# A router computed with its weights as the stationary operand, and its steps and the base downs in another order

## The reference

```
h = layernorm(x)*(1+ca) + sa
x = x + ga * (attention(layernorm(h)*gamma+beta) @ o_proj + h)      # causal, one head of 256
h = layernorm(x)*(1+cb) + sb
gate, up = h @ Wg.T, h @ Wu.T                                        # 704 wide
probs = softmax(h @ Wr.T); topw, topi = top_k(probs, 2)              # the router, 8 experts
out = silu(gate)*up @ Wd.T
for the two chosen experts e (LoRA rank 16, factor 2):
    he = silu(gate + lora_g[e](h)) * (up + lora_u[e](h));  out += topw[e] * lora_d[e](he)
x = x + gb * out
```

## Time and profile before

| | us |
|---|---|
| median of 3 runs | 688.92 (688.87 to 689.52) |
| time of the profiled execution | 688.73 |
| its span, first to last instruction | 686.9 |
| PE busy | 652.9 (95%) |
| DVE busy | 474.2 (69%) |
| ACT busy | 356.7 (52%) |
| POOL busy | 377.4 (55%) |

### The profile page before, as it was taken

One profiled execution on the slowest core, in us unless ns is written; L12 is line 12 of the kernel. 1 busy time (PEld: TensorE's weight loads), 2 busy tenths in 40 slices (PEclk: granted clock), 3 DMA queues, 4 the chain that ended last, 5 costly groups with the idle time before them and its releaser, 6 DMA issues.

```text
span 686.9 us, 10710 instructions
## 1 busy us (share of the span) xinstructions
PE 652.9 (95%) x3772; PEld 558.8 (81%) x3772; DVE 474.2 (69%) x1146; ACT 356.7 (52%) x642; POOL 377.4 (55%) x473
## 2 busy tenths in 40 slices
PE   4869999999999999999999999999999999999996
PEld 3559987888879987888878897798888998788885
DVE  5997678478886677658976767747987657637323
ACT  4635455546455546465455446564454546654543
POOL 3785345538577236647576516654765635543644
PEclk9989999999999999999999999999999999999999
DMA  8300020000000020000000001000000000000000
GB/s 311 122 1 1 1 62 0 1 2 31 0 2 31 1 62 0 1 1 32 0 1 32 1 1 62 0 1 18 15 1 1 32 1 1 0 1 1 31 0 32
DMA packets 14054, 15.45 MB, mean 22 GB/s; under 512 B 1328, under 2 KB 12720, under 8 KB 14000
## 3 DMA queue, kind: packets, MB, share of 16 engines
q1 hardware_dynamic: 14000, 14.76, 6.4%
HBM read 10.57 MB, written 4.19 MB: 21 GB/s over the span
## 4 chain that ended last, share of the span: by engine, by line
PE 82%; DVE 12%; issue 2%; POOL 2%; DMA 1%; ACT 1%; DVEq 0%; SPq 0%
PE ps L1263 76%; PE ps L1272 6%; DVE xr L856 2%; DVE hid L1103 1%; DVE rstd L829 1%; DVE zb L844 1%; DMA xs<-in_L_attn_x 1%; DVE xT_lo L890 1%; POOL ring_lo L469 1%; DVE mv L836 1%; DVE tr_full L856 1%; ACT act_s L709 1%; DVE zb L927 0%; DVE stat L841 0%; DVE nr_a L827 0%
## 5 line engine op out<-in xcount | busy, mean ns | idle before, releaser
L469 POOL TENSOR_TENSOR ring_lo<-hid,ring_hi 128x512 fp32r<-128x512 f32 x144 | 189.3, 1319 | 115.9 <-ACT ring_hi L717 115.2
L1103 DVE TENSOR_TENSOR hid<-act_s,ps 128x512 f32<-128x512 f32 x120 | 81.9, 684 | 82.0 <-ACT act_s L709 81.4
L709 ACT ACTIVATE act_s<-ps 128x512 f32<-128x512 f32 x120 | 71.7, 597 | 123.0 <-PE ps L1263 122.4
L717 ACT ACTIVATE ring_hi<-hid 128x512 fp32r<-128x512 f32 (+1 forms) x144 | 90.3, 627 | 16.2 <-DVE hid L1101 8.7
L461 POOL TENSOR_TENSOR xT_lo<-tr_full,xT_hi 128x512 fp32r<-128x512 f32 x28 | 35.9, 1297 | 33.5 <-ACT xT_hi L588 33.5
L1263 PE MATMUL ps<-wdT_hi,ring_hi 128*128 128x256 f32 x192 | 53.6, 285 | 0.0
L1263 PE MATMUL ps<-wdT_lo,ring_hi 128*128 128x256 f32 x192 | 53.2, 282 | 0.0
L1263 PE MATMUL ps<-wdT_hi,ring_lo 128*128 128x256 f32 x160 | 45.2, 282 | 0.0
L1263 PE MATMUL ps<-tm_hi,bgT_hi 128*128 128x512 f32 x96 | 39.5, 411 | 5.7 <-DVE hid L1103 5.7
L1263 PE MATMUL ps<-vv_hi,pT_hi 128*128 128x256 f32 x144 | 43.3, 301 | 0.0
L476 POOL TENSOR_TENSOR xr<-xr,y_gb 128x256 f32<-128x256 f32 x31 | 22.1, 739 | 34.2 <-DVE y_gb L1138 34.2
(11 more groups left out here) (229 smaller groups left out, 2026.4 us busy)
## 6 DMA issues: line engine op xcount, KB each, us to landing
xs<-in_L_attn_x SPq DMA_DIRECT2D x4, 1024.0 KB, 5.6
out<-xr SPq DMA_DIRECT2D x7, 512.0 KB, 3.0
s_mod<-in_L_wmod SPq DMA_DIRECT2D x1, 1024.0 KB, 8.8
s_qkvT<-in_L_attn_qkv SPq DMA_DIRECT2D x1, 768.0 KB, 10.3
s_wg<-in_L_ffn_Wg SPq DMA_DIRECT2D x1, 704.0 KB, 7.4
s_wu<-in_L_ffn_Wu SPq DMA_DIRECT2D x1, 704.0 KB, 8.6
s_wd<-in_L_ffn_Wd SPq DMA_DIRECT2D x1, 640.0 KB, 7.3
s_mod<-in_L_wmod SPq DMA_DIRECT2D x1, 512.0 KB, 6.9
```

The source lines that it names most:

```text
L469: pool.tensor_sub(ring[1][:, place(n), :], hid[:, n % HID, :], ring[0][:, place(n), :].bitcast(fp32)).then_inc(h_lo.sem, 1)
L709: nc.scalar.activation(act_s[:, n % 2, :], ps[:, 2 * (n % 2), :], ACT.Silu).then_inc(silu_ready.sem, 1)
L717: nc.scalar.activation(ring[0][p0:P, place(n), :], hid[p0:P, n % HID, :], ACT.Copy).then_inc(h_hi.sem, 1)
L1103: V.tensor_mul(hid[:, n % HID, :], act_s[:, n % 2, :], ps[:, 2 * (n % 2) + 1, :]).then_inc(h_ready.sem, 1)
```

## The change

- `logits(ci)` now takes `wr_both` as PE's weights (16 or 8 columns) and all 512 rows of the half as the moving operand: 4 matmuls where there were 16. The result has the logits on 16 partitions. ACT copies them to SBUF (`logits_copy`), and PE transposes them back in four transposes (`logit_transposes`), into another bank.
- First half: the transposes of `zb`, their scaling on DVE and the two `tr_high` on ACT move one turn up, into i = 7. PE's list is then: `logits(0)`, `adapter_inputs(0)`, `logit_transposes(0)`, the whole last `probs_values`, `mask(0, 0)`, half a base, `mask(0, 1)`, the other half. Before, `logits(0)` stood inside the last `probs_values`, and both masks behind the first half of the base.
- On DVE one `adapter_input_low` now stands before `router_shift(0)` and the other behind it; the statistics of rows 4 and 5 stand behind the masks.
- The block of `moments` and `rsqrt` behind hidden(5) is cut into pieces behind hidden(2), (3), (4) and (5).
- Second half's router: `logits(1)` stands behind both bases of group 2, its transposes behind the first adapter step; DVE's and ACT's steps move one or two units later.
- The base downs (slot 0) of groups 0 and 1 move behind the adapter downs of groups 0 and 1. `FILL` has the same counts, with what stood behind the last adapter step written as a fifth number.
- `spread_weights(1)` on ACT stands behind the two `adapter_input_high(1, .)`, and waits for the downs that free the places 6 and 7; `spread_masks(1)` waits for those that free place 4.

```diff
@@ -279,15 +281,15 @@
-        def down_order(ci, g):
...
-            slots = (0, 1, 2) if ci or g else (1, 2, 0)
-            return [(slot, a) for slot in slots for a in range(2)]
+        def downs(g, slots):
+            return [(g, slot, a) for slot in slots for a in range(2)]
+        DOWNS = (downs(0, (1, 2)) + downs(1, (1, 2)) + downs(1, (0,)) + downs(0, (0,)) + downs(2, (0, 1, 2)),
+                 downs(0, (0, 1, 2)) + downs(1, (0, 1, 2)) + downs(2, (0, 1, 2)))
...
-            ci, g, rest = q // UPC, q % UPC // 6, q % 6
-            slot, a = down_order(ci, g)[rest]
+            ci, rest = divmod(q, UPC)
+            g, slot, a = DOWNS[ci][rest]
@@ -308,9 +314,10 @@
         T_BANKS = ((4, 5), (0, 1))
-        MASK_BANKS = ((7, 6, 4, 5), (3, 4, 5, 6))
+        MASK_BANKS = ((6, 7, 4, 5), (3, 4, 5, 6))
         LOGIT_BANK = (2, 7)
-        PV_FIRST = TC
+        LOGIT_TR_BANK = (3, 6)
+        logit_rows = tr_full[0:2 * E, 0, :]
@@ -514,6 +521,7 @@
                             if r == 0:
+                                pool.wait_ge(pv_ready.sem, pv_ready.at(b, NT - 1))
@@ -664,6 +672,9 @@
                     scores_exp(i)
+                    if i == NT - 1:
+                        for k in range(KT):
+                            tr_high(b, KT * NC + k, xT[0][:, 0, k, :])
@@ -672,9 +683,11 @@
                             normalise(tile, zb[:, tile, :], xr[:, tile, :], z2_ready)
-                tr_high(b, KT * NC, xT[0][:, 0, 0, :])
                 probs_high(NT - 1)
-                tr_high(b, KT * NC + 1, xT[0][:, 0, 1, :])
...
+                def logits_copy(ci):
+                    act.wait_ge(logit_rows_ready.sem, logit_rows_ready.at(b, ci))
+                    nc.scalar.activation(logit_rows, ps[0:2 * E, LOGIT_BANK[ci], :], ACT.Copy).then_inc(logit_rows_copied.sem, 1)
@@ -689,7 +702,7 @@
-                        act.wait_ge(h_used.sem, h_used.at(b, down_position(unit(ci - 1, GROUPS - 1, 1, 1))))
+                        act.wait_ge(h_used.sem, h_used.at(b, freed(ci - 1, (RING - 2, RING - 1))))
@@ -721,9 +734,10 @@
-                router_exp(0)
+                logits_copy(0)
...
                     adapter_input_high(0, g)
+                router_exp(0)
@@ -734,7 +748,9 @@
                         silu(n0 + r)
-                        if ci == 0 and r == 14:
+                        if ci == 0 and r == 13:
+                            logits_copy(1)
+                        if ci == 0 and r == 15:
@@ -766,9 +782,9 @@
                     if ci == 0:
-                        spread_weights(1)
...
                         adapter_input_high(1, 1)
+                        spread_weights(1)
@@ -819,14 +835,18 @@
-            def rsqrt(lo, n):
+            def newton(lo, n, rounds):
                 v, a, y = nr_v[:, lo:lo + n], nr_a[:, lo:lo + n], rstd[:, lo:lo + n]
-                link(guess(lo, n))
-                for _ in range(NEWTON):
+                for _ in range(rounds):
...
+            def rsqrt(lo, n):
...
+                link(guess(lo, n))
+                newton(lo, n, NEWTON)
@@ -1006,19 +1026,19 @@
                         x1_stats(i - 3)
-                    if i == NT:
-                        ffn_scale(0, 0)
...
                         mark(V.reciprocal(rinv[:, t:t + 1], rowsum[:, t:t + 1]))
+                        if i == NT - 1:
+                            ffn_scale(0, 0)
...
                         queries_values(b, (6 + i,))
-                    if i >= 2:
+                    if 2 <= i < NT:
@@ -1027,7 +1047,7 @@
                 def router_shift(ci):
-                    logits = ps[:, LOGIT_BANK[ci], 0:TC * 2 * E].rearrange("p (t h e) -> p h t e", h=2, e=E)
+                    logits = ps[:, LOGIT_TR_BANK[ci], 0:TC * 2 * E].rearrange("p (t h e) -> p h t e", h=2, e=E)
@@ -1067,7 +1087,7 @@
-                        dve.wait_ge(h_used.sem, h_used.at(b, down_position(unit(ci - 1, GROUPS - 1, 1, 1))))
+                        dve.wait_ge(h_used.sem, h_used.at(b, freed(ci - 1, (RING - 4,))))
@@ -1141,17 +1161,18 @@
+                x1_product(NT - 2)
+                adapter_input_low(0, 0)
                 router_shift(0)
-                x1_stats(TC)
-                x1_stats(TC + 1)
+                adapter_input_low(0, 1)
...
                 spread_masks(0)
+                x1_stats(TC)
+                x1_stats(TC + 1)
+                x1_stats(TC + 2)
                 x1_product(NT - 1)
-                x1_stats(TC + 2)
-                for g in range(2):
-                    adapter_input_low(0, g)
@@ -1160,22 +1181,27 @@
                     hidden(r)
-                    if r == 5:
+                    if r == 2:
                         x1_stats(TC + 3)
+                    if r == 3:
...
                         mark(V.tensor_scalar(neg_mean[:, TC:NT], mv[:, TC:NT, 0], -1.0, None, ALU.mult))
-                        rsqrt(TC, TC)
+                    if r == 4:
+                        link(guess(TC, TC))
+                        newton(TC, TC, 1)
+                    if r == 5:
+                        newton(TC, TC, NEWTON - 1)
...
                         ffn_scale(1, 6)
-                    if r == 12:
+                    if r == 14:
                         router_shift(1)
-                    if r == 14:
+                    if r == 15:
                         router_probs(1)
-                    if r == 15:
+                    if r == 16:
                         router_top()
-                    if r == 16:
+                    if r == 17:
@@ -1385,12 +1411,6 @@
                             values(b, range(NT // 2 + 2 * i, NT // 2 + 2 * i + 2))
-                    else:
...
-                        for k in range(KT):
-                            pe.wait_ge(z2_ready.sem, z2_ready.at(b, TC - 1))
-                            pe.wait_ge(probs_ready.sem, probs_ready.at(b, NT - 2))
-                            transposes(b, KT * NC + k, k, k, [zb[:, tile, :] for tile in range(TC)])
@@ -1403,6 +1423,10 @@
                             last_mm.then_inc(pt_ready.sem, 1)
+                    if i == NT - 1:
+                        pe.wait_ge(z2_ready.sem, z2_ready.at(b, TC - 1))
+                        for k in range(KT):
+                            transposes(b, KT * NC + k, k, k, [zb[:, tile, :] for tile in range(TC)])
@@ -1412,12 +1436,18 @@
                     pe.wait_ge(tr_lo.sem, tr_lo.at(b, KT * NC + ci * KT + 1))
+                    for k in range(KT):
+                        x_hi, x_lo = inputs(ci)[k]
+                        mm(ps[0:2 * E, LOGIT_BANK[ci], :], wr_both[:, k, :, :].rearrange("p h e -> p (h e)"), x_hi, k == 0, False)
+                        last_mm = mm(ps[0:E, LOGIT_BANK[ci], :], wr_both[:, k, 0, :], x_lo, False, k == KT - 1)
+                    last_mm.then_inc(logit_rows_ready.sem, 1)
...
+                def logit_transposes(ci):
...
+                    pe.wait_ge(logit_rows_copied.sem, logit_rows_copied.at(b, ci))
                     for t in range(TC):
-                        o = ps[:, LOGIT_BANK[ci], 2 * t * E:2 * (t + 1) * E]
-                        for k in range(KT):
-                            x_hi, x_lo = [x_[:, t * P:(t + 1) * P] for x_ in inputs(ci)[k]]
-                            mm(o, x_hi, wr_both[:, k, :, :].rearrange("p h e -> p (h e)"), k == 0, False)
-                            last_mm = mm(o[:, 0:E], x_lo, wr_both[:, k, 0, :], False, k == KT - 1)
+                        last_mm = transpose(ps[:, LOGIT_TR_BANK[ci], 2 * t * E:2 * (t + 1) * E], logit_rows[:, t * P:(t + 1) * P],
+                                            ident[0:2 * E, 0:2 * E])
@@ -1474,14 +1504,15 @@
                     if slot == 0:
-                        if j == 0 and ci == 0:
+                        first = (g, slot, a) == next(d for d in DOWNS[ci] if d[1] == 0)
+                        if first and ci == 0:
                             pe.wait_ge(shifted_ready.sem, shifted_ready.at(b, 1))
-                        elif j == 0:
+                        elif first:
...
                                 last_mm = mm(ps[:, 6 + t // 2, t % 2 * D:(t % 2 + 1) * D], hn[ph][:, t * P:(t + 1) * P], wdT[pw][:, j, :],
-                                             j == 0 and t % 2 == 0 and (ph, pw) == (0, 0), False)
+                                             first and t % 2 == 0 and (ph, pw) == (0, 0), False)
@@ -1512,22 +1543,26 @@
-                FILL = {(0, 0): (0, 0, 0, 0), (0, 1): (0, 1, 1, 1), (0, 2): (2, 2, 2, 1),
-                        (1, 0): (0, 0, 0, 0), (1, 1): (1, 2, 1, 1), (1, 2): (1, 2, 1, 1)}
+                FILL = {(0, 1): (0, 1, 1, 1, 1), (0, 2): (2, 2, 2, 1, 1),
+                        (1, 1): (1, 2, 1, 1, 1), (1, 2): (1, 2, 1, 1, 1)}
...
-                    fill = []
+                    fill = [(ci, *d) for d in DOWNS[ci]]
...
+                    def downs_before(g, place):
+                        nonlocal fill
+                        count = FILL[ci, g][place] if g else 0
```

(35 more changed lines are left out.)

4 lines of the change are left out of this document (added).

## The result

The changed kernel takes 704.47 us (703.88 to 705.84, six runs) against 688.92 of the kernel before: a ratio of 1.0226, 95% interval 1.0212 to 1.0239. It is slower, as forecast, but by 15.5 us and not by 4.3, and outside the range. The profiled execution took 703.88 us, with a span of 702.1 (before: 686.9); the mean granted clock of the matrix engine fell from 0.994 to 0.984.

What follows compares the result with a forecast made beforehand. PE, busy 652.9 of 686.9 us, was taken as the bound. Per batch + 2.05 - 0.6 - 0.6 + 0.33 = + 1.2; four batches 4.7, less 0.35, gave + 4.3 on 688.92: 693.2 us, range 689.0 to 697.0.

Steps and rivals of the forecast that it cites:

- The new pause: PE, after the last value matmul, waits 2.4 us for DVE's pick_b before mask(0,0), in every batch.
- Stage F: PE from the last row's scores to the first base up: forecast 2.05 us later in each batch.
- DVE's chain: DVE's first-half router steps up to the end of pick_b, which the masks need: forecast 5.16 to 5.2 us.
- The cheaper logits of the first half: First-half router work on PE: 4 wide matmuls and 4 transposes take 1.38 against 1.78 us, 0.40 less.
- the rival in which the chain hides: At PE's wait for mask(0,0): DVE's router chain hides under the last value row, no wait; 683.7 us, chance 0.08.
- The clock rival: PE's clock falls to half speed in the new pause, losing 1.8 us a batch; 700.6 us, chance 0.07.
- what is left of the normalisation's wait: PE's wait around hidden(4) to hidden(6), second half's normalisation: 1.0 of 1.6 us left, gain 0.6 a batch.
- rival (a): DVE's small normalisation operations are not held by POOL, 0.15 us of the wait is left; 689.9 us, chance 0.20.
- The 0.35 extra in the fourth batch: Normalisation wait: batch 4 had 0.35 us more to lose, so 0.35 more is gained there once.
- The second half's logits: Second-half router on PE: 0.94 for matmuls plus 0.44 for transposes, 0.6 us less a batch.
- The spread weights: spread_weights(1) on ACT, moved before dsum_high, makes up_adapters(0) wait 0.33 us more a batch; bounds 0 and 0.66.
- The "no wait" for the base downs: Second half's router: base downs only change places among the same work, so PE gets no wait.

Runs made afterwards that it cites:

- the filled kernels: Changed kernel with nine, or five, unused 512-column matmuls on PE before the wait for mask(0,0): 699.98 us with nine, 699.75 us with five.
- experiment 9: Changed kernel with old front, one-block normalisation, spread weights behind dsum_high(0), and old order of first-half base downs and second-half transposes: 694.57 us.
- experiment 3: Changed kernel with the second half's logits put back between the two bases of group 2, ACT's copy one unit earlier: 702.71 us.
- experiment 2: Changed kernel with the second half's normalisation put back as one block behind hidden(5): 702.39 us.
- 4: Changed kernel with ACT issuing dsum_high(0) before spread_weights(1), as in the kernel before: 703.92 us.
- experiment 7: Changed kernel with the first half's order, the one-block normalisation and spread_weights(1) behind dsum_high(0) all put back: 685.95 us.

## Why the prediction was right or wrong

**Right.** The new pause: forecast 2.4 us, measured 2.45 from end to start, 2.29 marked. Stage F grew by 2.04 in the first batch, and by 2.05 in the batches of the filled kernels; forecast 2.05. DVE's chain from its first read to the end of `pick_b` took 5.16 (250.67 to 255.83); forecast 5.16 to 5.2. The cheaper logits of the first half: 0.43, forecast 0.40. So the rival in which the chain hides fell, and its opposite was rightly put first.

**Wrong: "the pauses of 1.5 us change nothing, and this one is 2.4".** The clock rival had 7 in 100, and it is what happened: three batches of four, 1.47 + 1.44 + 1.36 = 4.3 us (forecast of the rival: 1.8 each in all four, which is 7.2 and not the 7.4 that stands there). The fills show it by themselves: with PE kept at work and the masks at the same time, these 4.3 us come back. It isn't the whole miss; 693.2 + 4.3 is 697.5. My reasoning set a pause between a case without an effect (1.5 us) and one with an effect (34 to 40 us) and took it for the first. The second case was read too coarsely: PE's last work before it ends at 34.17, and in windows of 0.2 us the clock is at 1.00 up to 36.8 and at 0.50 from 37.0, so it fell under 3 us into the pause. A nearer case speaks the other way: in the set-up of the kernel before PE also stands for 3.08 us, and the clock stays at 1.00. But the same pause in the changed kernel, 2.62 us here, is followed by transposes of twice the cost, at a clock of 0.50 from 27.6 to 30.8:

```profile
27.98 1.06 PE L1272 MATMUL ps<-ident,xr 128*128 128x128 f32 x8 [3.08 <-DVE xr L856]
```

```profile
27.82 1.94 PE L1298 MATMUL ps<-ident,xr 128*128 128x128 f32 x8 [2.62 <-DVE xr L876]
```

Of the twelve profiled executions, ten lose the clock behind this pause and two (the kernel before and experiment 9) do not. So one trace could not exclude a fall in a pause of 2.4 us, and it belonged inside the range. It is not certain in a pause of this length either: one batch was spared in the profiled execution of the changed kernel, three in that of experiment 3, none in 2 and 4. The Trainium skill, TensorE: Matmul & The Clock Gate, section "What's actually happening", calls the transition at the start of a kernel run-variable. These traces show the same in the middle of one.

**Wrong: what is left of the normalisation's wait (1.0 of 1.6).** The layout by hand, with every operation held, gave 1.3; the measured gain of stage N is 0.23 a batch, so about 1.4 is what is left. I then took 1.0 because two of fifteen operations seemed thin evidence, and rival (a) had it that most of them last 0.16 "though POOL works beside some". That reading was wrong: in the trace before POOL stands idle from 266.40 to 267.91 and again from 269.20, and all the operations of 0.16 that follow `neg_mean` start there, but for one that starts 0.06 before POOL's end. What lay beside POOL was held, in all four batches. The rule of the Trainium skill, SBUF — State Buffer, section "Who interferes with whom", that such an operation is blocked for the whole of a GpSimd operation that started first, has every piece held, which was the 1.3. The trace agrees, with four held operations that end 0.01 or 0.02 behind POOL's. The 0.35 extra in the fourth batch did not come (18.16 to 17.93, as in the others). Together 0.9 us instead of 2.75 (0.8 in the table, where the second batch has 0.08 of the clock's loss in it).

**Missing: what stands behind on DVE.** I priced the split at its own wait only. In the first three batches the stretch behind it holds preparation of the next batch, and with the split `bc` lands on a POOL operation and takes 1.03 longer, `hidden(10)` is late behind it, and bases (0,2,0) and (0,2,1) wait (0.16 and 0.25 marked; 0.32 and 0.42 by the distances from the start before, less a matmul's own 0.23). Undoing the split takes 0.3 from G and 0.61 from L in these three batches, and nothing from L in the fourth, which has no next batch. That is 2.7 us that the prediction has not at all. In which of the two ways the lateness is passed on (through POOL's hold, or simply by DVE's order shifted by a microsecond) was not separated.

**Mis-sized.** The second half's logits: 0.41 a batch and 0.20 in the last (experiment 7 against before), forecast 0.6, so 1.0 us short. The four transposes cost 0.53 and not 0.44 (in experiment 7 the steps around them, 286.60 to 287.60, are 1.00, of which 0.47 are two steps of 0.235): PE's restart is paid on both sides of them. The rest, 0.1 a batch, was not traced. The spread weights: 0.44 and 0.12 behind it, forecast 0.33: 0.8 more. The "no wait" for the base downs was right, and the wait that appears without them (experiment 9) shows that moving them is a condition of the new form, which I had passed over in a sentence (the order of the downs and the place of the transposes were tested together).

The sum for the span: 4.3 forecast, + 4.3 clock, + 1.8 normalisation, + 2.7 behind it, + 1.0 logits, + 0.8 spread = 14.9 of 15.2.

## What to carry to other kernels

A small chain on another engine is priced by the work that lies between its start and its use, and moving the producer earlier gains nothing if the work that covered it is moved ahead of it as well: count what is left between them. A wait put into the matrix engine's queue can cost more than its length, since the clock behind it may be halved; keep long waits out, or break them with any work there is. Where a split of small operations is tried against a neighbour that holds them, cut once and place the pieces where the neighbour is idle, and read every later stage of the busy engine before believing the gain.

## What the runs showed of the hardware

- A pause of PE of 2.45 us was followed by about 3 us at a granted clock of 0.53 to 0.62 in windows of 2 us (0.50 in finer ones) in three batches of four (in profiled executions of experiments 2 and 4 in all four, of experiment 3 in one), at a price of 1.4 to 1.6 us each. With a marked wait of 1.13 or 0.26 us in the same place there was none. Length alone does not decide it: waits of 0.68 and 1.05 close together (experiment 9) were followed by a fall in one batch of four, and the 3.08 us in the set-up of the kernel before by none.
- The lowered stretch need not start with the pause's end. In the changed kernel's second batch PE starts again at 255.98 and the clock is at 0.50 from 256.2 to 259.4; in the fourth batch of experiment 2 PE starts again at 584.36 and the clock is at 0.50 from 585.6 to 588.8, so part of the price falls into the next stage.
- A matmul of 512 moving columns costs the same 0.235 us from start to start with 16 or 8 columns of weights as with 128:

```profile
291.32 0.40 PE L1289 MATMUL ps<-xT_hi,wr_both 128*16 128x512 f32 x1
291.56 0.39 PE L1289 MATMUL ps<-xT_lo,wr_both 128*8 128x512 f32 x1
```

- DVE operations of 4 columns, 0.16 us where POOL was idle, took 0.86 to 1.21 beside a POOL operation of 1.29 that had begun before them, and ended with it; a DVE operation of 512 columns took 1.72 instead of 0.69.
